# A decoder kernel's routed experts: hidden products transposed, each expert's matrices copied to fixed buffers, stage ends without GpSimd's drain

## The reference

```
def swiglu(x, w1, w2, w3):
    h = x @ w1
    return h * sigmoid(h) * (x @ w2) @ w3
gate_out = x @ gate_w                       # 8 experts
top_v, top_i = top_k(gate_out, 2)           # two for each row
w = softmax of the two, 0 for the other six
out = sum over e of swiglu(x, ew1[e], ew2[e], ew3[e]) * w[..., e]
out = out + swiglu(x, sw1, sw2, sw3)        # an expert shared by all rows
```

## Time and profile before

| what | us |
| --- | --- |
| runs (median first) | 2766.59, 2768.04, 2761.22 |
| the profiled execution | 2770.02 |
| its span, first to last instruction | 2768.2 |
| mean clock granted to TensorE | 0.963 of full |

### The profile page before, as it was taken

One profiled execution on the slowest core, in us unless ns is written; L12 is line 12 of the kernel. 1 busy time (PEld: TensorE's weight loads), 2 busy tenths in 40 slices (PEclk: granted clock), 3 DMA queues, 4 the chain that ended last, 5 costly groups with the idle time before them and its releaser, 6 DMA issues. The chain is left out here.

```text
span 2768.2 us, 95705 instructions
## 1 busy us (share of the span) xinstructions
PE 2516.4 (91%) x29950; PEld 2005.2 (72%) x29951; DVE 1814.5 (66%) x5178; ACT 1735.1 (63%) x6375; POOL 1396.5 (50%) x2914
## 2 busy tenths in 40 slices
PE   7999997899999999969888869999999799999995
PEld 6888886566666666648667757888888688888884
DVE  3555565566666666655333447888888488888886
ACT  4666664355555555412555647888888578888883
POOL 2333332233333333336676446777777266666664
PEclk9999999799999999979999989999999899999997
DMA  6323233111111111113232211111111111111100
GB/s 157 99 82 88 81 88 78 39 44 44 44 41 45 40 45 39 31 56 104 71 78 73 66 58 46 52 51 51 51 48 43 33 29 33 33 30 30 31 27 10
DMA packets 270160, 151.37 MB, mean 55 GB/s; under 512 B 51776, under 2 KB 263744, under 8 KB 270016
## 3 DMA queue, kind: packets, MB, share of 16 engines
q1 hardware_dynamic: 261312, 131.57, 17.8%
q0 software_dynamic: 8704, 17.97, 1.8%
HBM read 92.52 MB, written 48.51 MB: 51 GB/s over the span
## 5 line engine op out<-in xcount | busy, mean ns | idle before, releaser
L1576 ACT ACTIVATE pr<-psT 120x512 f32<-120x512 f32 (+1 forms) x512 | 277.9, 595 | 302.7 <-PE psT L1483 302.7
L1186 ACT ACTIVATE pr<-psS,small 128x128 f32<-128x128 f32 x1024 | 365.9, 383 | 96.0 <-DVE small L1257 93.4
L1621 DVE TENSOR_REDUCE small<-psS 128x4 f32<-128x992 f32 x256 | 303.5, 1186 | 93.4 <-PE psS L1487 93.4
L1473 PE MATMUL psT<-cross_Qm,cross_xf 32*120 32x512 f32 (+1 forms) x1024 | 307.4, 643 | 48.0 <-DVE cross_xoT L1669 43.5
L1186 ACT ACTIVATION_READ_ACCUMULATOR pr<-psS,small 128x1 f32 x1024 | 226.2, 221 | 0.0
L2163 POOL DMA_INDIRECT results<-experts_ob,experts_xb x144 | 138.5, 962 | 116.3 <-ACT experts_ob L1983 103.2
L1257 DVE TENSOR_REDUCE small<-psS 128x8 f32<-128x1024 f32 x128 | 156.8, 1225 | 61.6 <-PE psS L1151 61.6
L1478 PE MATMUL psS<-cross_xf,cross_Qm 32*128 32x248 f32 x1024 | 194.0, 430 | 0.9 <-DVE small L1621 0.9
L2103 DVE SCALAR_TENSOR_TENSOR experts_bgh<-experts_bth,psS 128x256 f32<-128x256 f32 x144 | 60.7, 421 | 199.1 <-ACT experts_bth L1975 199.1
L955 POOL TENSOR_SCALAR pr<-pr,small 128x120 f32<-128x120 f32 x512 | 179.1, 366 | 23.9 <-DVE small L909 23.9
L813 ACT ACTIVATE pr<-psS,small 128x120 f32<-128x120 f32 x512 | 178.6, 389 | 5.4 <-DVE small L928 5.4
(11 more groups left out here) (318 smaller groups left out, 7763.4 us busy)
## 6 DMA issues: line engine op xcount, KB each, us to landing
self_parts<-results SPq DMA_DIRECT2D x64, 192.0 KB, 2.4
slots<-blank SPq DMA_DIRECT2D x18, 520.0 KB, 4.7
experts_xb<-slots SPq DMA_DIRECT2D x144, 65.0 KB, 1.9
self_near<-in_x SPq DMA_DIRECT2D x128, 64.0 KB, 1.9
between<-self_xo SPq DMA_DIRECT2D x128, 64.0 KB, 1.6
cross_x<-between SPq DMA_DIRECT2D x128, 64.0 KB, 1.8
cross_res<-between SPq DMA_DIRECT2D x128, 64.0 KB, 1.8
self_x<-in_x SPq DMA_DIRECT2D x64, 64.0 KB, 1.8
```

Source lines behind the costliest of these rows:

```text
L1186: last = act.activation(pr[e.slot % 4][:, cols], K.S[e.slot % 2][:, cols], ACT.Exp, bias=nmax[e.slot % 4][:, n:n + 1], accum_out=tot[k.slo ...
L1473: pe.matmul(T[0:size, 512 * n:512 * n + 512], xf[t.slot][rows(g), every][:, places[ck]], Qm[t.slot][rows(g), :], start=True, stop=False)
L1576: act.activation(PT[k][0:sizes[ck], half], T[0:sizes[ck], half], ACT.Exp).then_inc(exped, 1)
L1621: dve.tensor_reduce(out, src, AX.X, ALU.max, negate=True).then_inc(maxed, 1)
```

## The change

What it does, part by part:

- The hidden products are turned round. For block b, `pick[b % 2]`, 512 columns in the second half of `K.pr[0]` or `K.pr[1]`, holds the expert's e1 (first 256) and e2 (last 256). Each product is two instructions with 128 columns of `pick` as weights and `xbT` moving, so the result has the hidden dimension down the partitions. The two transposes of `bgu` (L1938), the tiles `bguT` and ScalarE's copy (L1979) go; `bout` takes `bgu` itself.
- The copies to `pick` are new. VectorE lays down e1 of block a = b + 2 behind its two operations (`lay`, semaphore `picked`), ScalarE e2 behind the copy `xbT` (`picked2`). Each of them loads the expert's number for itself, in every step. TensorE waits for `picked` and `picked2`. Before the blocks, both wait for `owned`, with which `expert` is complete.
- TensorE needs the number for block t alone, for the third matrix. In the hardware loop the end of a step loads that of block b - 1, for the slots up to 6; slot 0 has to load block b - 2 as well.
- Every block is made with `no_gpsimd_drain=True`: its end has the other engines' drains and the barrier, and none of GpSimd. At the end of the experts GpSimd waits for all its transfers (`scattered[1]`, and `kept[0]` to `kept[7]`) and then issues `dma_reset()`.

The diff, without those six blocks whose line is the same as the first shown here:

```diff
@@ -126,7 +126,7 @@
         self.stale_holder.close()
         self.stale, self.stale_holder, self.signals, self.holder = self.signals, self.holder, [], ExitStack()
         if last:
-            with self.nc.Block() as block:
+            with self.nc.Block(no_gpsimd_drain=True) as block:
                 @block.gpsimd
                 def _(pool):
                     self.clear(pool)
...
@@ -1809,7 +1809,7 @@
         bth = [sb(f"bth{i}", [P, T]) for i in range(2)]
         bgh = sb("bgh", [P, T])
         bgu = [sb(f"bgu{i}", [P, 2, P]) for i in range(2)]
-        bguT = [sb(f"bguT{i}", [P, 2, P]) for i in range(2)]
+        pick = [K.pr[i][:, 512:1024] for i in range(2)]
         ob = [sb(f"ob{i}", [P, P]) for i in range(ring)]
 
         tern, ternq = ([K.pr[t][:, half * INNER:(half + 1) * INNER] for t in range(3)] for half in range(2))
@@ -1825,8 +1825,8 @@
         xb_in = [sem(f"xb_in{i}") for i in range(deep)]
         kept = [sem(f"kept{i}") for i in range(deep)]
         shared_out = sem("shared_out")
-        bT_ps, bT_sb, bgT_ps, bgT_sb, bh_ps, bhu_ps, bout_ps, btanhed, bopened, bgated, ob_sb = (sem(n) for n in (
-            "bT_ps", "bT_sb", "bgT_ps", "bgT_sb", "bh_ps", "bhu_ps", "bout_ps", "btanhed", "bopened", "bgated", "ob_sb"))
+        bT_ps, bT_sb, picked, picked2, bh_ps, bhu_ps, bout_ps, btanhed, bopened, bgated, ob_sb = (sem(n) for n in (
+            "bT_ps", "bT_sb", "picked", "picked2", "bh_ps", "bhu_ps", "bout_ps", "btanhed", "bopened", "bgated", "ob_sb"))
 
         W = K.W
         G, R = W[0], W[1]
@@ -1913,37 +1913,32 @@
                     held[b.slot] = pe.value_load(expert[0:1, bass.ds(b.n, 1)], min_val=0, max_val=EXPERTS)
 
                 def step(b):
-                    a, g, t, f = b + 2, b - 1, b - 2, b + 1
-                    looped = not isinstance(b.p, int)
-                    if b.slot == 0 or not looped:
+                    a, t = b + 2, b - 2
+                    if not looped(b) or b.slot == 0:
                         held.clear()
                     if b.live:
-                        if b.slot not in held:
-                            load(b)
-                        e = held[b.slot]
                         need(pe, bT_sb, b.done())
+                        need(pe, picked, b.done())
                         need(pe, bopened, (b - 2).done())
-                        pe.matmul(K.S[b.slot % 2][:, 0:T], xbT[b.slot % ring][:],
-                                  K.e1[:, bass.ds(e, 1), :].rearrange("p a f -> p (a f)"), start=True, stop=True).then_inc(bh_ps, 1)
-                        need(pe, bgT_sb, (b - 2).done())
-                        pe.matmul(K.S[b.slot % 2][:, 512:512 + T], xbT[b.slot % ring][:],
-                                  K.e2[:, bass.ds(e, 1), :].rearrange("p a f -> p (a f)"), start=True, stop=True).then_inc(bhu_ps, 1)
-                    if t.live and t.slot not in held:
-                        load(t)
-                    if looped and b.slot < deep - 1:
-                        load(f)
-                    if g.live:
-                        need(pe, bgated, g.done())
                         for blk in range(2):
-                            last = pe.transpose(K.S[g.slot % 2][:, 768 + blk * P:768 + (blk + 1) * P],
-                                                bgu[g.slot % 2][:, blk, :], K.ident[:])
-                        last.then_inc(bgT_ps, 1)
+                            last = pe.matmul(K.S[b.slot % 2][:, blk * P:(blk + 1) * P], pick[b.slot % 2][:, blk * P:(blk + 1) * P],
+                                             xbT[b.slot % ring][:], start=True, stop=True)
+                        last.then_inc(bh_ps, 1)
+                        need(pe, bgated, (b - 2).done())
+                        need(pe, picked2, b.done())
+                        for blk in range(2):
+                            last = pe.matmul(K.S[b.slot % 2][:, 512 + blk * P:512 + (blk + 1) * P],
+                                             pick[b.slot % 2][:, HID + blk * P:HID + (blk + 1) * P],
+                                             xbT[b.slot % ring][:], start=True, stop=True)
+                        last.then_inc(bhu_ps, 1)
                     if t.live:
+                        if t.slot not in held:
+                            load(t)
                         e = held[t.slot]
-                        need(pe, bgT_sb, t.done())
+                        need(pe, bgated, t.done())
                         need(pe, ob_sb, (t - 2).done())
                         for blk in range(2):
-                            last = pe.matmul(W[2 + t.slot % 2][:, 0:P], bguT[t.slot % 2][:, blk, :],
+                            last = pe.matmul(W[2 + t.slot % 2][:, 0:P], bgu[t.slot % 2][:, blk, :],
                                              K.e3[:, bass.ds(e, 1), blk, :].rearrange("p a n -> p (a n)"),
                                              start=(blk == 0), stop=(blk == 1))
                         last.then_inc(bout_ps, 1)
@@ -1951,6 +1946,8 @@
                         need(pe, bT_sb, (a - 2).done())
                         need(pe, xb_in[a.slot], a.landed())
                         pe.transpose(W[a.slot % 2][:, 0:P], xb[a.slot][:, 0:P], K.ident[:]).then_inc(bT_ps, 1)
+                    if looped(b) and b.slot < deep - 1:
+                        load(b - 1)
                 pipeline(pe, step, deep, nblocks, *bspan)
                 pe.wait_ge(totals, 4)
                 pe.wait_ge(bT_sb, nblocks)
@@ -1967,16 +1964,19 @@
                     act.activation(th[u.slot % 2][:], K.S[u.slot % 2][:, 0:2 * T], ACT.Tanh, scale=0.5).then_inc(tanhed, 1)
                 pipeline(act, shared, ring, pairs, 0, ring, pairs, pairs)
 
+                chosen = {}
+
+                def choose(b):
+                    chosen[b.slot] = act.value_load(expert[0:1, bass.ds(b.n, 1)], min_val=0, max_val=EXPERTS)
+
                 def step(b):
-                    a, g, t = b + 2, b - 1, b - 2
+                    a, t = b + 2, b - 2
+                    if not looped(b) or b.slot == 0:
+                        chosen.clear()
                     if b.live:
                         need(act, bh_ps, b.done())
                         need(act, bopened, (b - 2).done())
                         act.activation(bth[b.slot % 2][:], K.S[b.slot % 2][:, 0:T], ACT.Tanh, scale=0.5).then_inc(btanhed, 1)
-                    if g.live:
-                        need(act, bgT_ps, g.done())
-                        need(act, bout_ps, (g - 2).done())
-                        act.copy(bguT[g.slot % 2][:].rearrange("p b t -> p (b t)"), K.S[g.slot % 2][:, 768:1024]).then_inc(bgT_sb, 1)
                     if t.live:
                         need(act, bout_ps, t.done())
                         need(act, kept[(t - ring).slot], (t - ring).landed())
@@ -1986,6 +1986,12 @@
                         need(act, bT_ps, a.done())
                         need(act, bhu_ps, (a - 4).done())
                         act.copy(xbT[a.slot % ring][:], W[a.slot % 2][:, 0:P]).then_inc(bT_sb, 1)
+                        if a.slot not in chosen:
+                            choose(a)
+                        need(act, bhu_ps, (a - 2).done())
+                        act.copy(pick[a.slot % 2][:, HID:2 * HID],
+                                 K.e2[:, bass.ds(chosen[a.slot], 1), :].rearrange("p a f -> p (a f)")).then_inc(picked2, 1)
+                act.wait_ge(owned, 1)
                 pipeline(act, step, deep, nblocks, *bspan)
 
             @block.vector
@@ -2096,7 +2102,22 @@
                                                  in1=of_pair(x[:], t)[:, :, 0:P], op0=ALU.mult, op1=ALU.add).then_inc(added, 1)
                 pipeline(dve, shared, ring, pairs, 0, ring, pairs, pairs + 2)
 
+                chosen = {}
+
+                def choose(b):
+                    chosen[b.slot] = dve.value_load(expert[0:1, bass.ds(b.n, 1)], min_val=0, max_val=EXPERTS)
+
+                def lay(b):
+                    if b.slot not in chosen:
+                        choose(b)
+                    e = chosen[b.slot]
+                    dve.tensor_copy(pick[b.slot % 2][:, 0:HID],
+                                    K.e1[:, bass.ds(e, 1), :].rearrange("p a f -> p (a f)")).then_inc(picked, 1)
+
                 def step(b):
+                    a = b + 2
+                    if not looped(b) or b.slot == 0:
+                        chosen.clear()
                     if b.live:
                         need(dve, btanhed, b.done())
                         need(dve, bgated, (b - 1).done())
@@ -2104,9 +2125,12 @@
                                                  op0=ALU.add, op1=ALU.mult).then_inc(bopened, 1)
                         need(dve, bopened, b.done())
                         need(dve, bhu_ps, b.done())
-                        need(dve, bgT_ps, (b - 2).done())
+                        need(dve, bout_ps, (b - 2).done())
                         dve.tensor_tensor(bgu[b.slot % 2][:].rearrange("p b t -> p (b t)"), bgh[:],
```

(7 more changed lines are left out.)

12 lines of the change are left out of this document (6 added, 6 removed).

## The result

The changed kernel takes 2740.51 us (median of 4 runs, 2735.85 to 2742.45), the kernel before 2763.9 us (4 runs); the ratio is 0.9913, 95% interval 0.989 to 0.9936. That is 24 us less, with 18 to 30 in the interval. The forecast was 2751 us, 15.6 us less.

The account below looks back on a forecast made before the run. GpSimd's indirect DMAs bound the pairs; in later blocks TensorE's array and sequencer were equally full. -10.9 - 2.4 + 4 - 6.5 = -15.8 us from 2770.0 gave 2754.2, for the median 2751 us (range 2740 to 2767).

Parts of the forecast that it names:

- the ends: End of the experts stage: GpSimd's drain replaced by a reset taken at 0.5 us, -6.5 us (0 to -6.7).
- part 2: Later 70 blocks: ScalarE's chain, with its new load and copy, sets the pace at 1.80 us a step, -10.9 us.
- Rival A: Later blocks: ScalarE's loads cost nearer 0.5 us, TensorE's sequencer binds at 1.72 us a block, 2743 us; chance 0.14.
- the long steps: Later blocks: the longer steps at a turn's start, with extra loads on TensorE, would be gone, turns 14.8 us, not 16.06.
- TensorE's own bound of 14.2 to 14.6 a turn: Later blocks: 8 loads a turn on TensorE instead of 10, 1.46 us of 16.06 gone by its sequencer.
- The upper bound given beside the -10.9: Later 70 blocks: ScalarE's step at its upper end, 2.03 us a block, gives +2 us.
- Part 4: Tail and start: tail blocks from 2.14 to about 1.75 us, -2.4 us; start of the blocks 0, between +1 and -1.
- Part 5: The 64 pairs: VectorE's copies slow GpSimd's indirect DMAs by 0.07 us a pair, +4 us (0 to +21).
- rival C: Later blocks: VectorE's copy is held by GpSimd's indirect DMA, kernel slower, 2792 us at a 0.7 us wait; chance 0.09.
- w: Later blocks: VectorE's copy's wait for GpSimd's indirect DMA, up to 0.96 us; from 0.45 the kernel is above 2774.9 us.

Follow-up runs that it names:

- const_act_dve: The changed kernel without loads of the expert's number on ScalarE and VectorE (both copies take expert 0's matrices): 0.9860 of the kernel before, turn 13.40 us.
- const_all: The changed kernel without any load of the expert's number, expert 0 throughout: 2709.88 against 2764.94 us before (one execution), turn 11.70 us.
- both_on_act: The changed kernel with ScalarE making both copies with one load, VectorE none: 0.9904 of the kernel before on the long-gap chip, turn 14.08 us.
- ends_only2: The kernel before with only the stage ends changed (no GpSimd drain, waits for transfers, reset), measured again: 0.9966 of the kernel before, long-gap chip.

## Why the prediction was right in sign and too small in size

**Right.** The late stretch was limited by loads on TensorE's sequencer and shrank when they moved; pairs are GpSimd's and did not shrink; ScalarE and VectorE have their 144 loads each; the ends gave 6.0 us of 6.5, with the reset at 0.30 where I took 0.5, and VectorE's rounding late next; the other five stage ends gave nothing that can be told from the spread; tail -2.95 against -2.4.

**The step that failed is part 2,** "ScalarE's chain becomes the pace: 8 x 1.80 + 0.4". It failed in size and in mechanism. The later blocks gave 15.5 us and not 10.9, which is 4.6 of the 10.5 us between the table's two sums; the pairs (3.2) and the start (2.65) are nearly all of the rest. The size first. ScalarE's timeline of the changed kernel:

```profile
1526.49 0.38 ACT L1979 ACTIVATE experts_bth<-psS 128x256 f32<-128x256 f32 x1
1526.88 0.37 ACT L1983 ACTIVATE experts_ob<-psW,experts_xb 128x128 f32<-128x128 f32 x1
1527.15 0.26 ACT L1988 COPY experts_xbT<-psT 128x128 f32<-128x128 f32 x1
1527.73 0.40 ACT L1992 COPY pr<-e 128x256 f32 x1 [0.33 <-issue]
1528.04 0.38 ACT L1979 ACTIVATE experts_bth<-psS 128x256 f32<-128x256 f32 x1
```

`xbT` to copy, which holds the load, a wait and an address, is 0.58 us, and 0.58 to 0.72 over the 56 steps from 1500 to 1600 us, 0.62 on average. I had 0.93 (0.73 and 0.2), with 0.71 as the least. From the load's start to the copy's it is 0.63 to 0.74, so no 0.2 for a wait and an address came on top of the 0.73, and the load starts 0.04 us before `xbT` does. The other three distances, 0.27, 0.31 and 0.39, are as forecast, and the step, where nothing is waited for, is 1.55, the lower bound I gave (1.54). On VectorE the same term, from `bgu` to the copy, takes 0.83 to 0.87, close to the 0.92 taken there. The load's records on the three sequencers of the changed kernel, from 1500 to 1600 us:

```profile
L1970 ACTq TENSOR_LOAD <-experts_expert x56: 273/283/385, 1500.2 to 1598.7; - x56
```
```profile
L2108 DVEq TENSOR_LOAD <-experts_expert x56: 301/304/321, 1500.4 to 1599.1; - x56
```
```profile
L1913 PEldq TENSOR_LOAD <-experts_expert x56: 296/302/309, 1502.2 to 1599.2; - x56
```

The load itself costs the same on all three, 0.28 to 0.30 us. What I carried over was the price of a second and third load in a step that TensorE's array no longer covered, gaps of TensorE's sequencer included. Rival A had asked for "nearer 0.5 us" and gave 2743. It had the load's price about right and its time within 3 us, but not by its own path: it took 19 us from the later blocks, at 13.8 us a turn, and left the +4 of the pairs in; measured are 15.5, 14.32 and +0.8.

The mechanism: ScalarE's chain is not the pace. ScalarE waits for TensorE in 24 of 56 steps, and the turn is 14.32 us where its packed steps and the 0.4 would give 12.8. I had priced each engine by itself and taken the longest. All three came out near 1.6 us (TensorE 1.60, ScalarE 1.55, VectorE by the rows below 0.50, 0.83 and, where the copy isn't held, 0.3), and three nearly equal chains that hand on to each other through two slots did not run at the pace of any of them here. Alone, TensorE's loads give 13.40 and the others' 13.55; together 14.31, because the long steps of the two sides fall beside each other. So the long steps, which the forecast had gone, are still there. TensorE's own bound of 14.2 to 14.6 a turn was also too high, and at odds with the 1.70 and 1.72 us a block (13.6 to 13.8 a turn) that the same prediction used for TensorE in its bounds and in rival A. In const_act_dve a second load in a step costs 2.11 - 1.60 = 0.51 us and the first 1.60 - 1.45 = 0.15 over const_all: the array hides most of it. (The upper bound given beside the -10.9 is +1 and not +2 by its own terms: 70 x 2.03, less 3.1, less 138.)

**Part 4.** The start was worth -0.9 to -1.4, not 0: the first product no longer stands behind TensorE's loads, and VectorE's load and copy are done while the first block is still on its way. My bound was -1.

**Part 5.** +4 us was wrong in kind: 0.8 us in these traces, and by the second ones (pair 2.541 before, 2.545 after) 0.3. It is VectorE that yields. VectorE's timeline in the changed kernel:

```profile
1531.57 0.42 DVE L2114 COPY pr<-e 128x256 f32 x1 [0.42 <-issue]
...
1533.60 0.54 DVE L2114 COPY pr<-e 128x256 f32 x1 [0.42 <-issue]
1534.18 0.42 DVE L2124 SCALAR_TENSOR_TENSOR experts_bgh<-experts_bth,psS 128x256 f32<-128x256 f32 x1
1534.68 0.42 DVE L2129 TENSOR_TENSOR experts_bgu<-experts_bgh,psS 128x256 f32<-128x256 f32 x1
1535.51 0.29 DVE L2114 COPY pr<-e 128x256 f32 x1 [0.42 <-issue]
```

The same copy takes 0.29 or 0.54 us. So rival C had the right engine and the wrong size: w is at most 0.25 us and 0.06 on average (mean of the 144 copies 0.356, unheld 0.294), far from its 0.45. What the pairs do cost can't be told from the spread of two runs of one kernel (2.536 and 2.541 us before).

An estimate from the measured sides: had the turn been the longer of 13.40 and 13.55, the forecast would have been about 2740, which is the measured time by luck, since the real turn is 0.8 us longer and the pairs and the start made up for it. In part 2 itself two errors partly cancelled: ScalarE's step was taken 0.25 us too long, and what the engines cost each other was left out.

## What to carry to other kernels

Price a scalar load into a register by its records and by what covers it in the step where it stands; the extra length of a step with three of them is not its price. Where a change leaves three engines within 5% of each other, don't forecast the longest: here the coupled turn was 6% above either side. Look for the long step of each engine's loop, and whether the others' long steps lie beneath it or beside it. Three engines at 1.6 us also say where to look next, and moving work to the engine with the longest chain can still help (both_on_act); that it helps by taking a hand-over out of the loop is my reading, and no run isolates it.

## What the runs showed of the hardware

**A VectorE copy beside an indirect DMA of GpSimd is held in one narrow part of it.** Of the 130 copies of the changed kernel that start within an indirect DMA (0.96 us), those that start less than 0.50 us into it last 0.294 us, and so do those from 0.80 on. Those that start between 0.50 and 0.75 us end almost without exception 1.05 us after the DMA's start, whenever they began: at 0.55 they last 0.47, at 0.60 0.42, at 0.70 0.34. In all, 69 of the 130 were held. The other way round it is rarer: an indirect DMA that starts between 0.04 and 0.12 us after a copy did takes 1.00 to 1.07 us instead of 0.96 (two in the changed kernel, 27 of the 80 that start within a copy in const_all). ScalarE's copies of the same size take 0.404 to 0.407 us in the changed kernel, wherever they start. The Trainium skill, SBUF — State Buffer, section "SBUF: two separate sides", says that the one that starts first has the shared ports for its whole instruction and the other fully blocks; the rows show a hold of at most 0.25 us for the copy and 0.12 for the DMA, and none at all for copies that start in the other three quarters of the DMA's length. Here the measurement decides.

**GpSimd's drain at a block's end** took 11.14, 10.83 and 10.85 us behind the last indirect DMAs, with any units, and 0.91 at the end of a stage without them; the reset took 0.30, and no cost of it is seen in later stages.

**The long-gap chip.** There engines stand still for 5 to 20 us in the shared expert, put down to nothing but issue, with the same program and GpSimd scattering beside them. VectorE in ends_only2:

```profile
1269.38 0.69 DVE L2089 TENSOR_TENSOR experts_gu<-experts_gh,psS 128x512 f32<-128x512 f32 x1 [19.06 <-issue]
1270.01 0.42 DVE L2094 SCALAR_TENSOR_TENSOR routed_xT<-psW,routed_x 128x256 f32 x1
1279.72 0.69 DVE L2084 SCALAR_TENSOR_TENSOR experts_gh<-experts_th,psS 128x512 f32<-128x512 f32 x1 [9.29 <-issue]
```

The last shared result comes at 1374 to 1380 us instead of 1307, and a pair takes 3.12 (3.15 to 3.18 with the new units) instead of 2.54. In the later blocks, with no scatter left, the turns are within 0.4 us of the first chip's. What the engines wait for there stays open.
